# One instruction in place of two in the clamp of an absmax quantisation, inside an eight-layer transformer kernel on one Trainium2 core

## The reference, cut to what matters

```
def _absmax_act(x, eps=1e-5):
    scale = max(max(abs(x), axis=-1), eps) / 127.0
    return clip(round(x / scale), -128.0, 127.0) * scale

x = x + (einsum('bsi,oi->bso', _absmax_act(layernorm(x)), ternary(weight)) + bias)
```

## Time and profile before

| what | value |
|---|---|
| runs of the kernel before | 1106.76, 1107.0, 1107.4 us |
| profiled execution, device time | 1105.54 us |
| its span in the trace | 1103.5 us |
| granted TensorE clock, mean | 0.986 |
| DVE busy, of the span | 874.6 us (79%) |
| PE busy, of the span | 1025.0 us (93%) |

### The profile page before, as it was taken

One profiled execution on the slowest core, in us unless ns is written; L12 is line 12 of the kernel. 1 busy time (PEld: TensorE's weight loads), 2 busy tenths in 40 slices (PEclk: granted clock), 3 DMA queues, 4 the chain that ended last, 5 costly groups with the idle time before them and its releaser, 6 DMA issues.

```text
span 1103.5 us, 19047 instructions
## 1 busy us (share of the span) xinstructions
PE 1025.0 (93%) x6546; PEld 869.4 (79%) x6546; DVE 874.6 (79%) x2154; ACT 622.6 (56%) x1657; POOL 567.3 (51%) x412
## 2 busy tenths in 40 slices
PE   6999999999998899888878899999999999999988
PEld 5458888888887686556556888998889988999976
DVE  6448777776778956589999888888887898888885
ACT  1584344444333346677747566666767667765643
POOL 3146666668653243043435665646565475655640
PEclk9999999999999999989979999999999999999999
DMA  7003111110100010100000101010000101000201
GB/s 267 1 1 110 32 55 52 35 59 29 58 1 27 1 56 18 61 1 2 20 1 19 59 1 39 1 58 2 21 19 1 59 1 39 1 20 1 88 1 39
DMA packets 15007, 37.43 MB, mean 34 GB/s; under 512 B 1648, under 2 KB 6848, under 8 KB 14400
## 3 DMA queue, kind: packets, MB, share of 16 engines
q1 hardware_dynamic: 14912, 36.21, 9.7%
HBM read 35.16 MB, written 1.05 MB: 33 GB/s over the span
## 4 chain that ended last, share of the span: by engine, by line
PE 64%; DVE 23%; ACT 6%; issue 4%; POOL 2%; DMA 0%; DVEq 0%; SPq 0%; ACTq 0%; POOLq 0%
PE bank L737 15%; PE bank L759 8%; PE bank L2153 7%; PE bank L2176 7%; PE bank L2084 7%; PE bank L2059 3%; ACT y L2301 3%; PE bank L2095 3%; PE bank L1119 2%; DVE y L286 2%; DVE bst L249 2%; DVE g_ql L2018 2%; PE bank L2073 1%; PE bank L527 1%; DVE arena L1618 1%
## 5 line engine op out<-in xcount | busy, mean ns | idle before, releaser
L2301 ACT ACTIVATE y<-bank,g_mx 128x256 f32<-128x256 f32 x256 | 117.5, 486 | 97.6 <-DVE g_mx L2464 97.6
L2579 POOL TENSOR_TENSOR y<-y,g_sm 128x1024 f32<-128x1024 f32 x64 | 120.2, 1898 | 24.0 <-DVE g_sm L2477 24.0
L2555 POOL TENSOR_TENSOR g_c<-arena 128x1024 fp32r<-128x1024 f32 x30 | 64.1, 2137 | 116.3 <-DVE arena L2398 116.3
L2176 PE MATMUL bank<-arena 128*128 128x256 f32 x512 | 116.0, 379 | 0.0
L788 ACT ACTIVATE arena<-arena 128x512 f32<-128x512 f32 x64 | 40.5, 634 | 120.4 <-DVE arena L873 120.4
L2176 PEld LDWEIGHTS bank<-arena 128*128 128x128 f32 x512 | 94.9, 190 | 12.0 <-issue 0.2
L737 PE MATMUL bank<-b_yh,b_wh 128*128 128x512 f32 x256 | 100.6, 393 | 0.0
L737 PE MATMUL bank<-b_yl,b_wh 128*128 128x512 f32 x256 | 100.0, 391 | 0.0
L737 PE MATMUL bank<-b_yh,b_wl 128*128 128x512 f32 x256 | 99.7, 389 | 0.0
L2059 PE MATMUL bank<-cst,y 128*128 128x128 f32 x512 | 74.0, 277 | 17.7 <-DVE x L2386 14.6
L824 POOL TENSOR_TENSOR b_hl<-arena,b_hh 128x512 fp32r<-128x512 f32 x64 | 81.3, 1292 | 9.6 <-ACT b_hh L797 9.6
(11 more groups left out here) (384 smaller groups left out, 3153.4 us busy)
## 6 DMA issues: line engine op xcount, KB each, us to landing
arena<-in_dram SPq DMA_DIRECT2D x37, 512.0 KB, 3.5
arena<-in_dram SPq DMA_DIRECT2D x18, 256.0 KB, 3.9
arena<-in_dram SPq DMA_DIRECT2D x3, 1024.0 KB, 5.1
arena<-in_dram SPq DMA_DIRECT2D x2, 704.0 KB, 7.0
x<-in_dram SPq DMA_DIRECT2D x4, 256.0 KB, 5.5
cx<-in_dram SPq DMA_DIRECT2D x4, 256.0 KB, 5.6
cxT<-in_dram SPq DMA_DIRECT2D x4, 256.0 KB, 5.8
cx<-in_dram SPq DMA_DIRECT2D x1, 1024.0 KB, 6.1
```

The lines of the kernel that those rows point to most:

```text
L2176: m = pe.matmul(o[:, st * 256:st * 256 + 256], g_t[:, c, st * P:st * P + P], keys, start=True, stop=True)
L2301: m = act.activation(g_p[:, c, st, :], o[:, st * 256:st * 256 + 256], ACT.Exp, bias=g_mx[j % 2][:, 2 * c + st:2 * c + st + 1], accum_out=g ...
L2555: pool.tensor_tensor(cat, g_o[j % 2], g_om, ALU.subtract).then_inc(s_gc, 1)
L2579: pool.tensor_tensor(pf, pf, sums, ALU.mult).then_inc(s_gp, 1)
```

## The change

In `F_quant_dve`, for each of the four batches, two instructions become one. The new one reads `f_v` while it still holds the integer plus ROUND23, takes the minimum with ROUND23 + 127, subtracts ROUND23 and writes bf16 into `f_q`. ROUND23 + 127 = 12583039 is exact in float32. The maximum with -128 is gone, with one `V.sync()`.

```
             V.sync()
-            V.do(dve.tensor_scalar(f_v, f_v, ROUND23, -128.0, ALU.subtract, ALU.max))
-            V.sync()
             if b >= 1:
                 take(dve, ("F", "t", b - 1))
-            dve.tensor_scalar(f_q, f_v, 127.0, None, ALU.min).then_inc(s_fq, 1)
+            dve.tensor_scalar(f_q, f_v, ROUND23 + 127.0, ROUND23, ALU.min, ALU.subtract).then_inc(s_fq, 1)
```

## The result

The changed kernel has a median of 1106.64 us over 22 runs (1104.44 to 1108.36); the kernel before, on the same chips, 1108.22 us over 22 runs (1104.77 to 1109.95). The ratio is 0.9985 with a 95% interval of 0.9979 to 0.999, so 1.7 us less, with the interval from 1.1 to 2.3 us. The forecast was -1.86 us or 0.9983, inside that interval; the change is real and is within the 0.2% that the prediction called no change. The absolute 1105.1 us was 1.5 us too low. By the absolute number alone the result is nearer to rival A (1106.1) than to the forecast; which of the two it is, only the trace can say.

A forecast was written before the change was run, and what follows sets the result against it. DVE's dependent instructions were taken to bound the kernel at the four batches; removing four at 0.47 + 0.47 + 0.46 + 0.46 us gives -1.86 us, from 1107.0 to 1105.1 us (-0.17%). Range for 8 in 10 runs: 1102.8 to 1107.1 us.

The forecast's parts named there:

- rival A: A side path (ACT's exponentials, POOL's L2565) is as tight as DVE; two of four savings lost, 1106.1 us; chance 0.14.
- What bounds the kernel there.: Between 490 and 570 us DVE's dependent instructions, all four L1760 included, carry the chain and PE waits for them.
- What goes,: Four L1760, one per batch, each counted to the start of L1764: 0.47 + 0.47 + 0.46 + 0.46 = 1.86 us.
- The new instruction at the price of the old.: L1764 with a second arithmetic step, float32 in and bf16 out, still takes 427 ns, a cost of nothing.
- The 0.68 us of the upper bound: Longest duration considered for the new instruction, that of two-input L1796: 0.25 us more each, 1.0 us for four.
- The sides move along.: ACT, POOL and PE work beside the four batches moves with DVE; PE gains 0.45 us at batch 0, losing 0.02 at most.
- The air behind batch 3: Behind batch 3 POOL's L2565 ends at 559.41 us and DVE would be there at 559.75, leaving 0.34 us.
- Behind 570 us everything moves.: From 570 us on PE, ACT, DVE and POOL release one another and transfers move too, so the saving reaches the end.
- The sum.: Whole kernel: -1.86 us, to 1103.7 us against the profiled execution and 1105.1 us against the median of 1107.0.
- The clock.: Low clock, 566.1 to 576.3 us, costs 2.0 us at L2153, 0.41 us per us; a fall becomes a little less likely.
- D, a stretched instruction: Other work stretches the new DVE instruction; 0.47 us more each cancels the saving, 1.57 us each gives 1111.4 us; chance 0.02.
- B and C, the clock falling less or elsewhere: B: clock falls less, down to 1103.1 us, chance 0.18. C: falls elsewhere or more often, 1107.5 or 1109.3 us, 0.09.

The follow-up runs named there:

- experiment 3: Changed kernel with four more in-place minimum instructions in each of the four batches: 1113.24 us, ratio 1.0047 to the kernel before.
- experiment 4: Changed kernel with four more minimum instructions per batch, and 16 in place of 8 unread matmul passes ahead of batch 0's transposes: 1114.41 us, one execution.
- Experiments 1 and 2: 1: kernel before without the maximum with -128, two instructions kept, ratio 1.0006. 2: changed kernel without the upper bound too, 1104.85 us in one execution.
- experiment 5: Changed kernel with the row maximum taken over 16 of 256 columns: 1103.78 us in one execution.
- held before: Kernel before, its two instructions kept, with unread matmuls in two of PE's waits (12 and 8 passes): 1107.08 us, ratio 0.9991.
- experiment 8: Changed kernel with unread matmuls in five of PE's waits: 1103.89 us, ratio 0.9963 to the kernel before.

## Why the prediction was right

- *What bounds the kernel there.* Right. DVE carries the chain at all four places; adding four instructions per batch costs 1.84 to 1.85 us at three of them (experiment 3) and 1.87 at batch 0 once the clock is kept out (experiment 4, one execution).
- *What goes,* 1.86 us from start-to-start distances. Measured 1.88 over the stretch, and 0.48, 0.47, 0.46, 0.47 by batch. The forecast of the difference is no luck: it is four distances, and each came out.
- *The new instruction at the price of the old.* Right, 426 to 428 ns. The 0.68 us of the upper bound falls, and so does the estimate of 327 ns that the prediction drew from the Trainium skill, page "VectorE: DVE Perf Modes", section "The TRN2 errata — SBUF-src ops pay a fixed extra latency per instruction". Experiments 1 and 2 show that at this size and with these types neither the number of arithmetic steps nor the bound matters.
- *The sides move along.* Right for all four: PE's 0.45 us of waiting ahead of the first transposes is gone, POOL's L1554 still holds DVE for 1.50 us behind batch 1 and was moved with it. The air behind batch 3 was 0.33 us (POOL ends at 558.14 + 2.12 = 560.26, DVE starts at 560.59), forecast 0.34, and experiment 5 used it up. One side path was misread, PE's own: its 4.03 us of waiting were to shrink by about 0.46, and they stayed 4.03 (L1788), since the transposes ahead of them wait for batch 3's clamp too and move with it. Ahead of those transposes PE now waits 1.10 us where it had waited for nothing (L1774 at 560.44 us). PE is off the chain there, so the sum did not suffer.
- *Behind 570 us everything moves.* It can't be read from two profiles, since what follows L340 takes between 531.4 and 534.5 us in executions where nothing in it was changed. The 22 runs on either side say that the gain arrives: 1.7 us with an interval of 1.1 to 2.3.
- *The sum.* The difference was right. The base was taken from three runs, 1107.0, that lay closer together than the kernel's own spread of 5 us; that, and not the change, put the absolute forecast 1.5 us low.
- *The clock.* The price was right: 2.0 us were given to the low clock at L2153, and those 32 matmuls lose them when PE is kept busy (6.10 to 4.10 us). The rate too: in the changed kernel the clock rose again at about 574.1 us, so they ran for 2.2 us at low clock and took 0.88 us longer than 4.10, or 0.40 us for each, where 0.41 was forecast.

```profile
574.00:575.00 1.00, 1.00 (x10) 0.94 0.00 0
```

  The reason for a less likely fall was wrong, since the wait of 4.03 us got no shorter and one of 1.10 us came up ahead of it; the changed kernel's profile has the fall all the same. (L340's wait did shrink, from 3.58 to 2.43 us, since PE's work ahead of it ran on low clock.) The band of about 0.6 us around the forecast was too narrow: three runs 0.64 us apart stood for a kernel whose 22 runs spread over 5 us. The clock goes with that spread: of the 47 runs of the kernel before that were timed beside the experiments, the 38 with a mean granted clock of up to 0.980 have a median of 1108.8 us, and the 5 with 0.983 to 0.985 one of 1106.5. In the 22 runs of the changed kernel it is less plain; the longest, 1108.36 us, has 0.983. Where the low clock falls counts as well as how much of it there is.
- *Rivals.* A, part of it swallowed: refuted by the four segments. D, a stretched instruction: not for the new one, but one stood in the trace all the time a few lines earlier, at L1751 with 0.62 us for two columns, and I had not asked why. B and C, the clock falling less or elsewhere: the whole gained 1.7 us, with an interval that holds 1.88, so on average they came to little. That the change leaves the clock alone isn't shown, though. The three profiles with the two instructions (before, experiment 1, held before) all have low clock between 550 and 560 us, and none of the seven with the one instruction has; and the five of these seven that lack the dummy matmuls of experiment 8 all have low clock between 590 and 600, against one of the three. No run here separates this from chance.

## What to carry to other kernels

Where a chain of dependent small instructions on one engine sets the time, count instructions and not arithmetic: what a removed one gives back is the distance from its start to the next one's start, here 0.47 us each, and a second step in a TENSOR_SCALAR of 128x512 float32 cost nothing. Judge so small a change by the distances between the same instructions in both traces, not by the spans, and its effect on the whole by many runs on either side. And read an instruction that is far too long for its size as a wait, even if the profile marks no idle time before it; ask what the other engines do until it ends.

## What the runs showed of the hardware that I had not expected

- A wait of PE can cost more than itself, through the clock: at batch 0 a wait of 1.83 us, where the changed kernel has none, was followed by a granted clock of 0.63 and 0.51, and DVE waited 0.95 us in turn, a loss of 1.25 us on top of the 1.87; with 8 more unread passes of matmuls the loss was gone (one execution each). Not every wait does it: the kernel before waits 1.77 us ahead of its L1477 at 497.90 us, and the clock stays at 1.00 behind it.
- Filling a wait in part wasn't seen to help: with 2.09 us of it left the clock fell again, and the ratio was 0.9982 against 0.9985. With more passes in that wait, 0.79 us of it left, and three more waits filled, it was 0.9963. Which of the five places gave how much, no run tells.
- A two-column DVE instruction beside a POOL addition of 128x512 was held until that ended: 0.17 us without it, 0.62 and 1.12 us with it for the same L1751, by how early it starts.
